# Four indirect transfers in flight at most: a landing wait ahead of GpSimd's gathers and matrix writes

## The reference

```python
# layer 0, graph part: four message passes, k = 0..3
e = edge_attr @ eW[k] + eb[k]
m = relu(y[src] + e)
agg = segment_sum(m, dst)              # N rows of 256
h = relu(((1 + eps) * y + agg) @ W1 + b1) @ W2 + b2
# layer 1, graph part: attention over relations (8 heads)
h_src = h_all[edge_type, src]
w = exp(leaky(score_src + score_dst) - amax[dst])
out = segment_sum(h_src * w, dst) / segment_sum(w, dst)
# layers 2 and 3, graph parts: dense products with a weighted adjacency matrix A[src, dst]
```

## Time and profile before

| | us |
|---|---|
| median of 3 runs | 4588.18 (4584.67 to 4588.41) |
| the profiled execution | 4581.3 |
| its span, first to last instruction | 4579.6 |
| PE busy | 2819.1 (62%) |
| PE weight load busy | 2325.5 (51%) |
| DVE busy | 2228.5 (49%) |
| POOL busy | 1874.5 (41%) |
| ACT busy | 832.3 (18%) |

### The profile page before, as it was taken

The page is one execution under the profiler, slowest core; times in us unless marked ns, Lnnn a source line. Parts: engine busy times, 40 slices in busy tenths (PEclk is TensorE's granted clock), DMA queues, the critical chain, the costliest instruction groups (busy, mean ns, idle before and its releaser), DMA issues. The chain is left out here.

```text
span 4579.6 us, 54274 instructions
## 1 busy us (share of the span) xinstructions
PE 2819.1 (62%) x16062; PEld 2325.5 (51%) x16063; DVE 2228.5 (49%) x5468; ACT 832.3 (18%) x2163; POOL 1874.5 (41%) x1982
## 2 busy tenths in 40 slices
PE   3566646665666656650568346666769639947392
PEld 3455535554455445540556223346758539936382
DVE  7655645555555545566245547761254421144113
ACT  1122212222222222210112000002200113300020
POOL 4366546663666366636214667701200020020212
PEclk8788878887788877875769667767989769978696
DMA  6633323331333233312523133317756449945593
GB/s 156 225 91 90 84 61 89 90 90 54 89 91 89 52 90 90 91 31 105 182 56 95 48 94 94 94 39 254 243 196 233 140 171 329 308 155 176 178 339 127
DMA packets 358103, 607.68 MB, mean 133 GB/s; under 512 B 82185, under 2 KB 240187, under 8 KB 355131
## 3 DMA queue, kind: packets, MB, share of 16 engines
q1 hardware_dynamic: 245816, 357.76, 23.8%
q0 software_dynamic: 88640, 214.25, 16.7%
q10 hardware_dynamic: 23363, 32.26, 2.1%
HBM read 508.28 MB, written 95.81 MB: 132 GB/s over the span
## 5 line engine op out<-in xcount | busy, mean ns | idle before, releaser
L833 POOL DMA_INDIRECT gine_got<-gine_table,src x1056 | 1022.3, 968 | 601.7 <-issue 260.9
L893 PE MATMUL gine_p_sum<-gine_hot,gine_got 128*128 128x128 f32 x4224 | 837.8, 331 | 560.5 <-ACT gine_got L901 249.0
L893 PEld LDWEIGHTS gine_p_sum<-gine_hot,gine_got 128*128 128x128 f32 x4224 | 703.3, 236 | 707.8 <-issue 648.5
L922 DVE TENSOR_TENSOR gine_got<-gine_got,gine_p_edge 128x256 f32<-128x256 f32 x1056 | 437.2, 415 | 613.8 <-PE gine_p_edge L884 407.4
L901 ACT ACTIVATE gine_got<-gine_got 128x256 f32<-128x256 f32 x1056 | 439.0, 417 | 1183.3 <-issue 634.0
L488 POOL DMA_INDIRECT adjacency<-value,place x264 | 281.2, 1065 | 392.3 <-POOLq L54 185.0
L930 DVE TENSOR_TENSOR stack_acc<-stack_acc,gine_p_sum 128x256 f32 x1056 | 435.0, 412 | 3.9 <-issue 0.7
L883 PE MATMUL gine_p_edge<-gine_w_a,edge_space 128*128 128x256 bf16 x1056 | 335.3, 317 | 42.8 <-issue 34.8
L1398 PE MATMUL ffn_p_h<-ffn_xt,ffn_w 128*128 128x128 f32 x2864 | 345.8, 279 | 2.1 <-DMA ffn_w<-in_L_ffn_w 1.6
L1398 PEld LDWEIGHTS ffn_p_h<-ffn_xt,ffn_w 128*128 128x128 f32 x2864 | 336.2, 195 | 4.0 <-DMA ffn_w<-in_L_ffn_w 2.9
L884 PE MATMUL gine_p_edge<-gine_w_b,edge_space 128*128 128x256 bf16 x1056 | 334.4, 317 | 0.0
(11 more groups left out here) (399 smaller groups left out, 3345.3 us busy)
## 6 DMA issues: line engine op xcount, KB each, us to landing
gcn_a<-adjacency SPq DMA_DIRECT2D x270, 320.0 KB
ffn_w<-in_L_ffn_W SPq DMA_DIRECT2D x74, 1024.0 KB
ffn_w<-in_L_ffn_w SPq DMA_DIRECT2D x60, 1024.0 KB
ffn_w<-in_L_ffn_w SPq DMA_DIRECT2D x90, 512.0 KB
adjacency<-zero_row ACTq DMA_DIRECT2D x3, 7200.0 KB, 43.6
gine_got<-gine_table,src POOLq DMA_INDIRECT x1056
h_table<-score_rows SPq DMA_DIRECT2D x15, 1056.0 KB
edge_space<-dst_lines ACTq DMA_DIRECT2D x3, 2816.0 KB
```

The source lines that it names most:

```text
L833: pool.indirect_dma_start(got[:, c % RING, :], None, table, bass.IndirectOffsetOnAxis(ap=rows[:, c:c + 1], axis=0)).then_inc(gathered[c % ...
L893: ins = nc.tensor.matmul(p_sum[d % 4][:, half * P:(half + 1) * P], got[:, d % RING, half * P:(half + 1) * P], hot[:, d % HOTS, :], start=T ...
L922: nc.vector.tensor_tensor(got[:, c % RING, :], got[:, c % RING, :], p_edge[c % 4][:, 0:D], ALU.add).then_inc(summed, 1)
```

## The change

A constant `NEAR` = 4 is added. In the two loops of gathers, GpSimd waits before gather c (from c = 4 on) until gather c - 4 has landed. The matrix writes get four semaphores in place of two, and each write from the fifth on waits until the write four ahead of it has landed. `arrived` waits for all four. Transfers, their sizes and their order are the same.

```diff
+NEAR = 4
@@ class Adjacency
-        self.sent = [nc.alloc_semaphore(f"adjacency_sent{n}") for n in range(2)]
+        self.sent = [nc.alloc_semaphore(f"adjacency_sent{n}") for n in range(NEAR)]
@@ send
             if c == 0:
                 pool.wait_ge(self.blanked, 64)
+            if c >= NEAR:
+                pool.wait_ge(self.sent[c % NEAR], 16 * (c // NEAR))
             pool.indirect_dma_start(self.tables[c % 2], bass.IndirectOffsetOnAxis(ap=self.place[:, c:c + 1], axis=0),
-                                    self.value[:, c:c + 1], None).then_inc(self.sent[c % 2], 16)
+                                    self.value[:, c:c + 1], None).then_inc(self.sent[c % NEAR], 16)
@@ arrived
-        for n in range(2):
-            eng.wait_ge(self.sent[n], 16 * (EC // 2))
+        for n in range(NEAR):
+            eng.wait_ge(self.sent[n], 16 * (EC // NEAR))
@@ gather_rows
+        if c >= NEAR:
+            pool.wait_ge(gathered[(c - NEAR) % RING], 16 * ((c - NEAR) // RING + 1))
         if c >= RING:
             pool.wait_ge(used, c - RING + 1)
         pool.indirect_dma_start(got[:, c % RING, :], None, table,
@@ attend_in_order
+                if c >= NEAR:
+                    pool.wait_ge(gathered[(c - NEAR) % HELD], 16 * ((c - NEAR) // HELD + 1))
                 if c >= HELD:
                     pool.wait_ge(agg_done, c - HELD + 1)
                 pool.indirect_dma_start(got[:, c % HELD, 0:FULL], None, h_table,
```

More of the change, by code:

```diff
@@ L32 @@
 RING = 24
+NEAR = 4
 HOTS = 12
 LN_EPS = 1e-5
-assert EP * EJ == E and EC * P >= E + T * (P - 1) and EC % U == 0 and U % G == 0 and EC % RING == 0
+assert EP * EJ == E and EC * P >= E + T * (P - 1) and EC % U == 0 and U % G == 0 and EC % RING == 0 and EC % NEAR == 0
 class Phase:
```

## The result

The changed kernel takes 4640.06 us (median of 4 runs, 4631.64 to 4653.51), the kernel before beside it 4586.69 (4584.67 to 4588.41). The ratio is 1.0119, with a 95% interval of 1.0094 to 1.0145: 53 us slower. 4658 was predicted, with a range of 4582 to 4730.

The account below looks back on a forecast made before the run. GpSimd's gather issue plus its ring-slot pauses was taken to bound the passes. 52 (message passes) + 15 (attention) + 3.5 (`rank`) = +70 on 4581.3: 4652, or 4658 for the median; range 4582 to 4730.

Parts of the forecast that it names:

- The mechanism: Message and attention gathers: landing wait stays on the gather; ring wait `agg_done` becomes the sequencer's, some 960 and 220 rows.
- 0.4 us a pause: Message and attention passes: each pause of GpSimd for a ring slot gets 0.4 us longer behind the sequencer's wait.
- +13 a pass: Each message pass: 47 pauses x 1.26 in place of 53 x 0.86, +13 us, +52 for four.
- 90 raw and 52 left: Four message passes: raw price 56 pauses x 0.4 = 22 us a pass; +52 after chunks done in longer pauses.
- Attention, +15,: Attention pass: 41 pauses costing 0.76 each in place of 45 at 0.36, 31 us in place of 16, +15.
- Nothing changes: Rival, passes: chunk work sets the pace, later gathers after pauses cost nothing; +0 to 4 us, 4590; chance 0.23.
- Faster: Rival, passes: longer pauses free more chunk work held up by close gathers; -28 and -5 us, 4559; chance 0.11.
- Landing waits of gathers: 0: Gather loops: the fourth gather ahead has landed before its wait is reached, cost 0; upper bound 0.3 us a gather, hidden.
- Landing waits of writes outside rank: 0: Matrix writes outside `rank`: DMA share falls to 0.00 2.2 us after the last write's issue, so waits cost 0.
- Rank: +3.5: Matrix writes in `rank`: waits under ScalarE's loads cost +3.5 us, between bounds of nothing added and +15.6.

Follow-up runs that it names:

- e12: Kernel before, padding spread; passes 1, 2 gather three chunks ahead; 2, 3 wait for the first gather, then ring; 4 ring wait, then limit of four: 4753.91 against 4593.37.
- e8: Kernel before with only the padding rows of the matrix writes spread to cells 1056 bytes apart: 4292.65 against 4328.94, ratio 0.9917.
- e1: Changed kernel with the ring wait ahead of the landing wait in message passes and attention: 4349.63 against 4326.95 of the kernel before, ratio 1.006.
- e10: Kernel before with gathers limited to four in flight, ring wait first, landing wait second; matrix writes as before: 4332.39, ratio 1.0007.
- e9: Kernel before plus a wait for the very first gather ahead of the ring wait, no limit on transfers: 4329.53, ratio 1.0.
- e7: The changed kernel without an edit, run again beside the kernel before: 4647.78 against 4593.89, ratio 1.0119.
- e6: Changed kernel with eight matrix writes in flight in place of four, gathers still limited to four: 4633.0, 14.8 under the unedited changed kernel.
- e5: Changed kernel with padding rows of the matrix writes sent to cells 1056 bytes apart: 4600.7, ratio 1.0017 to the kernel before.
- e2: Changed kernel without the gathers' landing waits, so only the matrix writes wait for the fourth one ahead: 4343.16, ratio 1.0049 to the kernel before.

## Why the prediction came out as it did

- **The mechanism** is as predicted. Of two waits ahead of one instruction the second has rows of its own and the first has none: before, 1056 on line 921 and 112 on line 1395, none on lines 920 and 1394. So the ring wait moved to the sequencer (960 and 220 rows), the fourth pass of e12 shows that moving it back removes the loss under the same limit, and its third that the move alone makes it.
- **0.4 us a pause** was an estimate that no run shows: the 0.60 of the earlier trace rows less the 0.24 of the earlier trace rows, rounded up. It was nearly right: the first two passes of e12 differ by 0.48 a pause. Why GpSimd starts later behind the sequencer's wait no trace tells. The two kernels compared show the same difference themselves. Of the 170 pauses in the message passes of the kernel before, 159 end 0.26 us after a recorded signal `agg_done`; of the 226 in the changed kernel, 216 end 0.74 us after one.
- **+13 a pass.** The second pass did as forecast (+12.4), but the four together gave 35.4 in place of 52. The mis-sized term is the number of pauses and what comes back of them. The 56 of the earlier trace rows were not 56 pauses: the view also counts ordinary gaps of 0.30 us in which some signal happens to arrive. In e8, whose passes have no pause at all, it counts 46:

```profile
POOL gine_got L833 <- PE gine_p_sum L893: 14.0, 46, 0.3
```

- Counted as gaps of over 0.45 us between gathers, the second pass had 42 pauses, and all four had 170 of 248.6 us in all. The changed kernel has 226 of 309.6. The long ones (over 0.8 us) went from 151 of 1.57 us to 138 of 1.87, so fewer and longer, as forecast. But the short ones went from 19 to 88, which the forecast did not have: where the signal came just in time for a gather, it now comes too late. Above the usual 0.30 us the pauses grew by 44 us, and the passes by 35, where 170 pauses of 0.48 more would be 82. So more came back than I had counted (I had 90 raw and 52 left). My reading, which no run tests, is that a gather that starts late finds the next slot free already.
- **Attention, +15,** was +7.1. The 57 pauses of the earlier trace rows were 21 by the same count; they became 32, and above 0.30 us each they grew by 7.7 us. It was not taken apart by itself, but with its waits as before it takes 434.3 and (in e12) 435.5, and 439.0 to 441.4 in the four kernels with the changed ones.
- **"Nothing changes" and "Faster"** are out where there are pauses. The first holds fully where there are none. That I did not see: I read the pace of the passes as a property of the kernel. In e8 the same gathers without pause go with 1.29 us a chunk (224 in 290 us) at a clock of 1.00, where the earlier trace rows show 4 chunks in 24 us:

```profile
637.00:927.00 290.00, 92.77 (x224) 1.00 0.36 102
```

- In this row the DMA share is 0.36, as in the stretch with 4 chunks in 24 us, and the chunk work keeps up with the gathers. So gathers in flight do not slow the chunk work by themselves.
- **What holds the chunk work in the sets with pauses** can be read from the signal records. TensorE's signals stand there microseconds behind the matmuls that give them. Of VectorE's 349 additions (L922) that had to wait in the kernel before, from the 25th chunk of each pass on, 325 start within 0.03 us of a recorded `edge_done`, while their own matmul (L884) had ended 3.5 us earlier in the median. No pause of GpSimd ends less than 3.3 us after the sum that it waits for has ended (median 5.1). For the gather below that sum is the first row, which ends at 691.04; a signal `agg_done` is recorded at 695.95, 0.26 us ahead of the gather:

```profile
690.43 0.61 PE L893 MATMUL gine_p_sum<-gine_hot,gine_got 128*128 128x128 f32 x4
...
696.21 0.94 POOL L833 DMA_INDIRECT gine_got<-gine_table,src  x1 [1.59 <-PE gine_p_sum L893]
```

- In the sets without pauses all but at most one of the 1055 to 1057 recorded `edge_done` of each trace's passes stand within 0.05 us of a matmul's end; in the kernel before it is 104 of 941. The traces with pauses also hold only 26931 to 32031 of the 46128 signals that the issued DMAs give (16 each), the others 46018 to 46071. So nearly every pause ends with a late signal of TensorE. (The ends of matmuls are modelled, in both kinds of set alike.) In the first two passes of e12, a run with pauses where a gather goes out only every 1.75 and 1.95 us, the signals that GpSimd waits for are in time: 0.27 and 0.75 us are counted from the matmul's end. Why the signals are late in some sets, and what the closeness of the gathers has to do with it, is open; nothing here tells whether the recording of the trace has a part in it.
- **Landing waits of gathers: 0.** Right within about 2 us a pass: pass 4 of e12 takes 405.2. In e1 and e10, which have the limit and no ring pauses, two to four gaps a pass are longer than 0.45 us (0.7 to 1.0 us in the mean of a pass), and e10's passes are 2 us longer than e9's beside it.
- **Landing waits of writes outside rank: 0.** Wrong, +6.6 (and +11 in e7). I took 2.2 us from the moment at which the DMA share falls to 0.00 behind the last write. That row shows when packets are out of the engines, not when the transfer is signalled. The landing records of the same trace have the last signals of that write at 2606.05, 7.7 us after its start at 2598.32. A landing must be read from its semaphore.
- **Rank: +3.5** was +8.9. The 3.5 was an estimate between two bounds, 5.5 us late under the loads less 2.0 of cover, and no run shows it: GpSimd comes 5.9 late under the loads and 3.1 more at write 108, and the 2.0 did not come to bear: in both kernels the barrier comes 3.9 us after the end of GpSimd's last write, so GpSimd's end set the phase's already in the kernel before, where VectorE's comes 1.9 us ahead of the barrier. e6 and e5 show both causes.
- **Landings of matrix writes** take 2.14 us for write 100, 7.9 for write 104 with no packets but those of matrix writes under way, and 2.15 for the same write with the padding spread. ScalarE's waits for SyncE's stores are up to 8.7 us beside GpSimd's crowded padding writes and up to 4.7 beside spread ones. What makes crowded cells slow, and what ties those stores to them, no run shows.

## What to carry to other kernels

Where two waits precede one instruction, ask for the one that comes last first. In this kernel it then stayed on the gather, and a pause ended 0.27 us after the matmul in place of 0.75 (e12, medians of the first two passes); the other, over when reached, cost nothing measurable in the sequencer (240 of them in the fourth pass of e12, 405.2 us against 404.3 to 406.7 before). Send padding of a scatter to cells far apart, not to neighbours: 1056 bytes in place of 4 took 36 us off the kernel before (e8), and other engines' stores gained too (ScalarE's waits for them 56.7 us in place of 76.1). Read how long a transfer takes from its signals, never from the end of its packets: the last matrix write's packets were out 2.2 us after its start, its last signals came at 7.7. Count pauses by the gaps between instructions; a count of waits by releaser holds ordinary gaps too (46 of them, none over 0.3 us, in a pass of e8).

## What the runs showed of the hardware

- Of two waits ahead of one instruction, the second has a row `EVENT_SEMAPHORE` on its own line and the first none: x1056 on L921 and x112 on L1395 in the kernel before, x960 on L837, x220 on L2237 and x66 on L490 in the changed one.
- A gather starts 0.27 us after the end of TensorE's matmul when the wait for it is its own, and 0.75 us after when that wait is the sequencer's (e12, medians of 261 gathers in each of the first two passes). From the recorded signal it is 0.26 us in the kernel before and 0.74 in the changed one.
- Writes of 128 single floats land in 2.1 us with little else under way (write 100 of the changed kernel: 2.14). With 65 or more rows to neighbouring 4-byte cells they take 7.7 to 8.8 us (e1 and e2, whose records of the matrix writes are nearly complete). In the kernel before the last signals come 7.7 us after the start of the last of seven such writes.
- ScalarE's waits for stores on another queue fall from 76.1 to 56.7 us when the padding is spread, and the phase is 29 us shorter (e9 and e8).
- One kernel, unchanged, has message passes of 405 or of 352 us, whole sets of runs alike, on the same chip too, with a granted clock of 0.81 or 1.00 in the middle of a pass. In the slower kind TensorE's `edge_done` is recorded 3.5 us after its matmul in the median of the 325 additions that start on it in the kernel before, in the other all but at most one within 0.05 us. The cause is not known.
